# A stage of its own for the gates of a scan, with one bank for sums of reads and three for side work

## What is computed

```python
xr, gate = jnp.split(x @ W_in.T, 2, axis=-1)
xr = xr + t_emb[:, None, :]
xc = silu(conv(xr, W_conv) + b_conv)              # 4 taps along the tokens
xn = layernorm(xc) * ln_g + ln_b
Bm, Cm, dt = jnp.split(xn @ W_xproj.T, 3, axis=-1)
...
def step(h, inputs):
    ad, bd, xt, ct = inputs
    h = jnp.clip(h * ad[:, :, None] + bd[:, :, None] * xt[:, None, :], -10.0, 10.0)
    yt = jnp.einsum('bd,bdh->bh', ct, h)
    return (h, yt)
_, ys = jax.lax.scan(step, h0, ...)
y = ys.transpose(1, 0, 2) + D * xn
return y * jax.nn.silu(gate) @ W_out.T
```

## Time and profile before

| | us |
|---|---|
| median of 3 runs | 6171.38 (6165.83 to 6179.17) |
| the profiled execution, its own time | 6177.47 |
| its span, first to last instruction | 6175.7 |
| first step of the scan begins | 3330.83 |
| last step of the scan begins | 6085.6 |

### The profile page before, as it was taken

How to read it: one execution, slowest core, us unless ns; L and a number is a source line. 1 busy time by engine, 2 the same in 40 slices (tenths; PEclk the granted TensorE clock), 3 DMA queues, 4 the chain that set the end, 5 groups by cost and what they waited for, 6 DMA issues and landing times.

```text
span 6175.7 us, 73238 instructions
## 1 busy us (share of the span) xinstructions
PE 5759.9 (93%) x24000; PEld 2733.8 (44%) x24000; DVE 4481.3 (73%) x5676; ACT 2408.7 (39%) x4698; POOL 3215.3 (52%) x2625
## 2 busy tenths in 40 slices
PE   7999999999999999999986879899999999999998
PEld 3444444444444444444443424444444444444444
DVE  4656656556566565665536999999989999989984
ACT  2444444445444444444453414333342424334111
POOL 1876767677667776776644333425243443524213
PEclk7999999999999999999988889999999999999999
DMA  2332323332232322323214343544444453444433
GB/s 86 89 92 69 100 74 93 91 88 86 79 96 78 98 81 74 98 76 86 91 48 128 84 116 99 141 101 131 109 119 130 117 137 90 137 101 130 116 96 118
DMA packets 411565, 613.30 MB, mean 99 GB/s; under 512 B 58768, under 2 KB 189968, under 8 KB 410672
## 3 DMA queue, kind: packets, MB, share of 16 engines
q1 hardware_dynamic: 374320, 558.24, 32.5%
q10 hardware_dynamic: 36864, 50.38, 3.2%
HBM read 305.31 MB, written 201.38 MB: 82 GB/s over the span
## 4 chain that ended last, share of the span: by engine, by line
PE 67%; DVE 19%; issue 6%; ACT 2%; ACTq 2%; DMA 2%; POOL 1%; DVEq 1%; SPq 1%; POOLq 0%
DVE g L2093 9%; PE bank L786 8%; PE bank L816 8%; PE bank L774 6%; PE misc L803 5%; PE miscb L1832 5%; DVE g L2099 5%; PE xps L1807 5%; PE miscb L1862 4%; PE yps L1822 4%; PE miscb L1764 3%; PE bank L745 3%; PE bank L727 3%; PE bank L755 3%; PE bank L803 2%
## 5 line engine op out<-in xcount | busy, mean ns | idle before, releaser
L1127 POOL TENSOR_TENSOR acc<-acc,prob 128x512 f32<-128x512 f32 x1536 | 1908.1, 1281 | 841.2 <-PE bank L816 571.2
L1056 DVE TENSOR_REDUCE mx<-bank 128x1 f32<-128x512 f32 x2048 | 1307.5, 684 | 538.7 <-PE bank L786 532.4
L2093 DVE SCALAR_TENSOR_TENSOR g<-xps,bd,g 128x1024 f32<-128x1024 f32 x1024 | 1312.9, 1282 | 111.4 <-PE xps L1807 84.1
L1807 PE MATMUL xps<-sx,spread 128*128 128x512 f32 x2048 | 890.3, 520 | 193.9 <-DVE g L2093 180.5
L949 ACT ACTIVATE prob<-misc 128x512 f32<-128x512 f32 x1277 | 713.5, 598 | 751.4 <-PE misc L803 667.8
L786 PE MATMUL bank<-khat,qhat 96*128 96x512 f32 x2048 | 939.4, 519 | 13.2 <-DVE xt_s L1033 8.0
L2099 DVE TENSOR_SCALAR g<-g,lim 128x1024 f32<-128x1024 f32 x1024 | 899.2, 878 | 34.9
L1807 PEld LDWEIGHTS xps<-sx,spread 128*128 128x128 f32 x2048 | 357.7, 194 | 679.3 <-issue 358.4
L803 PE MATMUL misc<-qhat,khat 98*128 98x512 f32 x1443 | 604.1, 461 | 16.9 <-ACT prob L949 10.7
L786 PEld LDWEIGHTS bank<-khat,qhat 96*128 96x128 f32 x2048 | 373.1, 191 | 540.8 <-issue 382.3
L1822 PE MATMUL yps<-g,cexp 128*32 128x512 f32 x4096 | 517.4, 625 | 0.0
(11 more groups left out here) (221 smaller groups left out, 7212.6 us busy)
## 6 DMA issues: line engine op xcount, KB each, us to landing
sx<-scratch_xhl SPq DMA_DIRECT2D x512, 128.0 KB, 4.9
scratch_dx<-dx SPq DMA_DIRECT2D x64, 512.0 KB, 3.5
scratch_xhl<-xhi SPq DMA_DIRECT2D x64, 512.0 KB, 5.3
scratch_xhl<-xn SPq DMA_DIRECT2D x64, 512.0 KB, 5.6
scratch_y<-ysb SPq DMA_DIRECT2D x512, 64.0 KB
early<-scratch_dx SPq DMA_DIRECT2D x59, 512.0 KB, 6.2
early<-scratch_y SPq DMA_DIRECT2D x59, 512.0 KB, 4.3
xt_n<-in_x SPq DMA_DIRECT2D x112, 256.0 KB, 3.0
```

What stands on the lines that cost most here:

```text
L1056: dve.tensor_reduce(self.mx2[:, h * TT + qt, c:c + 1], bank[m][:, 0:QC], AX.X, ALU.max).then_inc(sem[f"dve_m{m}"], 1)
L1127: pool.tensor_tensor(self.acc[:, a, h, :], self.acc[:, a, h, :], self.prob[:, (n % 2) * GH + h, :], ALU.add).then_inc(sem["pool_acc"], 1)
L1807: mm = pe.matmul(self.xps[t % 2][:, half * BANK:(half + 1) * BANK], self.spread[:, 2 * part + half, :], self.sx[:, n % 2, wd, :], start=Tr ...
L2093: dve.scalar_tensor_tensor(self.g[:, t % STATES, :], self.xps[t % 2][:, :], self.bd[:, i % 2, tl:tl + 1], self.g[:, (t - 1) % STATES, :], ...
```

## The change

Four things are changed in the scan part, and nothing in the attention part but line numbers.

1. The gates of chunks 0 to 6 leave `finish` and get a lane of their own, `gate_rows(i)`. It runs from 0.34 of chunk i to 0.2 of chunk i + 1, so it no longer waits for the chunk's end. A gate is made in `sg`, stored to a new DRAM tensor (`stg`, 512 KB for one sequence), and loaded again by `finish` (`lg`) into a new buffer `sgl`, from which POOL multiplies.
2. The sums of `out` use one bank, 2. The other, 3, joins the side work: `SIDE` = (0, 1, 3). `out` of a unit's first half now waits until ACT has copied the unit before.
3. `expand` lays out 16 steps in one POOL operation instead of 8, `PACE_LATE` is 16 instead of 12, and the ends of three lanes are moved (`convolve` to 0.625, `rows` from 0.138 to 0.92, `finish` to 1.04 chunks).
4. Constants are loaded on one semaphore, on which all engines wait for all eleven loads; the scratch for DMA descriptors is 512 instead of 2048.

```diff
+WIDE = 16
+FINISHED = 1.04
+GATES = (0.34, 1.2)
...
-PACE_LATE = 12
+PACE_LATE = 16
...
-    SIDE, ALL = (0, 1), (0, 1, 2, 3)
+    SIDE, ALL = (0, 1, 3), (0, 1, 2, 3)
...
+    def gate_rows(i):
+
+        out = []
+        put = lambda *a, **k: out.append(item(*a, **k))
+        for b in range(B):
+            had = (i, b - 1) if b else (i - 1, B - 1)
+            was = lambda kind, *at: ((kind, *had, *at),) if i or b else ()
+            gone = () if i or b else tuple((kind, tt) for kind in ("f_st", "f_sT") for tt in (NCH - 2, NCH - 1))
+            put("SP", 0.6, ("fg", i, b), was("gm", 1, HT - 1) + gone, [("ld_gx", 16)], lands=3.0)
+            for half in range(2):
+                g = ("gm", i, b, half)
+                for it in range(HT):
+                    put("PE", 0.88, ("gm", i, b, half, it), (("fg", i, b),), [("pe_m{m}", 1)] if it == HT - 1 else [],
+                        take=SIDE if it == 0 else None, group=g)
+                put("ACT", 0.6, ("go", i, b, half), (("gm", i, b, half, HT - 1),) + was("stg"), [("act_m{m}", 1)], group=g,
+                    give=True)
+            put("SP", 0.6, ("stg", i, b), (("go", i, b, 1),), [("st_g", 16)], lands=4.0)
+        return out
+
     def finish(i, banks, room, batches):
...
                 if not final:
...
-                    put("SP", 0.6, ("fg", i, b, room), was("gm", 1, HT - 1) + gone, [(f"ld_gx{room}", 16)], lands=3.0)
-                    for half in range(2):
-                        g = ("gm", i, b, half, room)
-                        for it in range(HT):
-                            put("PE", 0.88, ("gm", i, b, half, it, room), (("fg", i, b, room),),
-                                [("pe_m{m}", 1)] if it == HT - 1 else [], take=banks if it == 0 else None, group=g)
-                        put("ACT", 0.6, ("go", i, b, half, room), (("gm", i, b, half, HT - 1, room),) + was("fs", end=1),
-                            [("act_m{m}", 1)], group=g, give=True)
-                gate = ("zo", b, 1) if final else ("go", i, b, 1, room)
+                    put("SP", 0.6, ("lg", i, b), (("stg", i, b),) + was("fs", end=1), [("ld_g", 16)], lands=4.0)
+                gate = ("zo", b, 1) if final else ("lg", i, b)
...
-                m = 2 + n % 2
+                m = 2
...
-        order.lane(expand(i, range(1, TOK // 8)), t - 4.0, t + 0.84 * TOK)
+        order.lane(expand(i, range(1, TOK // WIDE)), t - 4.0, t + 0.84 * TOK)
         if i + 1 < NCH:
-            order.lane(convolve(i + 1, SIDE), t - 1.0, t + 0.62 * TOK)
-            order.lane(rows(i + 1, SIDE), t + 0.2 * TOK, t + 0.93 * TOK)
+            order.lane(convolve(i + 1, SIDE), t - 1.0, t + 0.625 * TOK)
+            order.lane(rows(i + 1, SIDE), t + 0.138 * TOK, t + 0.92 * TOK)
         if i:
-            order.lane(finish(i - 1, SIDE, 0, range(B)), t + 1.0, t + TOK + (1.0 if i < NCH - 1 else -3.0))
+            order.lane(finish(i - 1, SIDE, 0, range(B)), t + 1.0, t + (FINISHED * TOK if i < NCH - 1 else TOK - 3.0))
+        if i < NCH - 1:
+            order.lane(gate_rows(i), t + GATES[0] * TOK, t + GATES[1] * TOK)
...
+        self.sgl = sb("sgl", [P, DIN])
...
+            elif kind == "stg":
+                i, b = at
+                for half in range(2):
+                    self.of_bank(w, "act", ("gm", i, b, half), ("go", i, b, half))
+                sp.dma_start(d["gate"][b, i * TOK:(i + 1) * TOK, :], self.sg[:, :]).then_inc(sem["st_g"], 16)
+            elif kind == "lg":
+                i, b = at
+                w.wait_ge(sem["st_g"], plan.after("st_g", ("stg", i, b)))
+                had = room_before(i, b, 0, self.NCH, B)
                 if had:
...
+                    w.wait_ge(sem["pool_y0"], plan.after("pool_y0", ("fs", *had, 0, 1)))
+                sp.dma_start(self.sgl[:, :], d["gate"][b, i * TOK:(i + 1) * TOK, :]).then_inc(sem["ld_g"], 16)
```

108 lines of the change are left out of this document (53 added, 55 removed).

## The result

| | before | after |
|---|---|---|
| median of four runs, us | 6172.0 | 6140.7 |
| lowest and highest, us | 6165.8, 6179.2 | 6133.9, 6146.2 |
| profiled span, us | 6175.7 | 6139.2 |
| attention part ends (first `q`), us | 3330.8 | 3324.1 |
| first chunk | 326.3 | 328.6 |

The ratio is 0.9948, with a 95% interval of 0.9931 to 0.9966. The forecast of 6058 (6025 to 6130) missed: the sign was right, the size was not. The first and the last chunk did what was forecast (+2.3 and -19.4 us). The six middle chunks, which were to give 100 us, gave 13.6. The 6.8 us of the attention part are no effect: its code did not change, and over the profiles of this case it ended anywhere from 3319.8 to 3341.6 us.

A forecast was written before the change was run, and what follows sets the result against it. Bound: DVE in the scan's first chunk, PE and DVE nearly full in the middle, PE in the last. Terms -79 - 21 - 23 + 2 + 8 = -113 took 6177.5 to 6064.5, at the median 6058 us; range 6025 to 6130.

The forecast's parts named there:

- What bounds it, and the price of a gap: Scan: DVE must wait when PE work between two inputs of steps goes over 4.34 us.
- Term 1: Middle chunks: balance and third bank cut DVE's waits from 19.7 to 6.5 us a chunk, -79 us.
- Term 2: Middle chunks: fewer unpaced POOL pieces overlap DVE's g, 3.5 us a chunk, -21 us.
- Term 3: Last chunk: 48 gm leave it, PE falls to 260 us and DVE becomes the bound, -23 us.
- Term 4: First chunk: the 48 gm are done there, DVE covers them and the clock should rise, +2 us.
- Term 5: Gate stores and loads in the scan: 56 each of 512 KB, SP queueing mostly hidden, +8 us, bounds 0 and 40.
- Inputs waiting for their DMA: Sign in the profile after: inputs seen waiting for their DMA would break a step of the prediction; no size given.
- Term 6: Single bank of sums, constants and tail: put at nothing.
- Waits move and do not go: Rival, DVE's waits: only those on pj shrink (-35), half of the overlap gain comes; -58, 6113 us, chance 0.20.
- Collisions on the ports: Rival, shared POOL and DVE ports: fs and wide expand run into g, up to 196 us, 6254; slower side 0.06.
- a stall at the bank: Rival, one bank of sums: out waits for ACT with inputs behind it, 166 us, 6224 us, chance 0.03.

The follow-up runs named there:

- the 8 us: Changed kernel with the planner counting 8.0 us in place of 3.0 from issue to landing of x2T_t's load: 6071.9 us, ratio 0.9849.
- the other numbers mended: Changed kernel, x2T_t's load ahead of the gate store, planned landings 6.0 us for x2T_t and 8.0 for x2T_sb, proj pass 1.2 us: 6026.6 us.
- two parts of 16 and 30 us: Kernel before with the new banks alone: 0.9974; changed kernel with x2T_t's landing planned at 8.0 us and the banks as before: 0.9951.

## Why the prediction was wrong, step by step

**What bounds it, and the price of a gap: right.** PE's in-order queue makes DVE wait where over 4.34 us of work stands between two inputs. At the place shown, two inputs in hand and 4.60 us of standing made DVE wait 3.69.

**Term 1, middle chunks (-79): the step that failed.** It held that DVE's waits would fall from 19.7 to 6.5 us a chunk; they rose to 24.6. It laid prices of PE's pieces on the queue and took it that each piece can start when PE comes to it. The order shows no landing. Here one of the pieces, `gm`, waits 23 times in six chunks, for 63.5 us, and mending that alone gives 61 us of time. The waits on `proj` and `x_t` fell by 43 us, as its measure of the first and second place has it (0.34 us is what is left at the second; 4.1 in place of 2.6 at the first). The part for `xps` came out at +50. The plan itself has the same fault: `scan_plan` gives a middle chunk 352.9 us before and 338.0 after, and measured are 353.7 and 351.4; with the 8 us it gives 338.5, and measured are 341.4.

The load is not all of it. With it mended by the plan alone DVE still waits 14.4 us a chunk, so the term's -79 is -32, and the time came within 20 us of the forecast 113 partly by luck, because `g` gave 39 us instead of 21. What was left stood before `xps` (43.9 us), `proj` (28.4) and ACT's results (12), and PE waited 14.2 us for `x2T_sb`, a second landing that the plan had too short. With the other numbers mended DVE waits 6.3 us a chunk, beside the 6.5 that the term held, but in another order of instructions than the one it was read from: that the two agree proves nothing for the term.

**Term 2, overlap of POOL and DVE (-21): the sign right, the reason half right.** `g` fell by 6.4 us a chunk, not 3.5. The step scaled it by the unpaced pieces, 9 in place of 17; the `g` that took over 0.86 us fell further, from 74 to 32 in six chunks. It is the reach of the pace that lowers it, as the step had it; the wider pieces alone give nothing. That a longer reach makes work late was not priced at all. On the kernel before it costs 2.1%, on the changed kernel, together with the wide pieces, it gains 0.5%. That the spread of the row work makes the room for it is likely, but no run has the reach of 16 without that spread and with the gates in their lane. The third bank is not needed for it: with two banks and the 8 us the changed kernel is still 0.5% under before.

**Term 3, last chunk (-23): right**, 19.4 us. PE is busy 271.5 us, not below 265, and the chunk is 289, not 285; DVE waits 4.9 us for inputs where 4 were held.

**Term 4, first chunk (+2): right**, 2.3 us, and the granted clock rose from 0.87 to 0.90.

**Term 5, stores and loads of gates (+8, bounds 0 and 40): right as a price of traffic, wrong as a price of the queue.** DMA's share is 0.51, near the 0.54 worked out, and where no load is late by it, it costs nothing that can be measured. The step named what stands on SP behind a waiting `stg`: loads of inputs, stores of y. It left out the load that its own lane puts right behind `stg`, that of `x2T_t`, and so missed who waits for that. "Inputs waiting for their DMA" was named as a sign that would break a step. It was meant for the inputs of steps, which did not wait. The input of `gm` did. The price of this queueing, 61 us, stands in neither term 1 nor term 5; it is over the 40 us that term 5 had as its bound.

**Term 6, at nothing: right.** No wait for the single bank of sums stands among PE's waits. The tail is 91.0 us against 90.0.

**The rivals.** "Waits move and do not go" was the nearest, with 6113 and a chance of 0.20; it assumed that waits for inputs stay at 45 us, and they doubled. It had the outcome's shape without the cause, so its price was too small, and the range ended at 6130 for that reason. Collisions on the ports and a stall at the bank did not come.

## What to carry to other kernels

An order says when an engine comes to an instruction, not when the instruction's operand is there. When a change adds or moves a transfer, list what is issued right behind it in the same queue and who waits for that: here 29 MB of stores and as many of loads were free in themselves, and the one 256 KB load that stood behind bursts of them took two thirds of what was won (61 of 93 us, by the ratios). A planned landing time should be read from the trace at the place where the load will stand, with what is issued ahead of it. And parts that look like separate gains may only pay together: two parts of 16 and 30 us made 93, and one piece of the second, the long reach with the wide pieces, is 31 of these 93 although it costs 1.7% on the kernel before.

## What the runs showed of the hardware

- A load of 256 KB issued from SP landed in 3.1 us (median of 41) with at most 256 KB issued in the 3 us ahead of it, in 3.5 to 3.8 us (11 of 12) behind one store of 512 KB alone, and in 6.9 us (median of 30, 5.0 to 9.8) behind over 1.2 MB. A load of 2 KB behind three transfers of 512 KB let its reader start 7.4 us after its issue.
- 59 MB more of traffic in the scan, at a DMA share of 0.51 of the time in place of 0.45, moved the time by nothing measurable once every reader had room for its landing.
- A `g` takes 812 ns (median). All 82 that took over 860 ns in the kernel before overlapped a POOL operation. Holding more POOL pieces back for a paced slot cut the sum of `g` by 3.4 us a chunk; making the pieces twice as long moved it by +1.4 us at the reach of 12 and by -2.3 us at 16.
- The untouched attention part differed by up to 21.8 us between profiled executions (3319.8 to 3341.6 us), more than several effects in this study. Sums by stage are the safer comparison.
